# The folded rope weights of a decoder layer: block-structured 128x128 matmuls against four 64x64 tiles of the TensorE array

## The reference, cut to what matters

```python
q_hk = (hidden_q @ Wq.T).reshape(B, S, H=16, K=128)
q_big = einsum('bshk,hkq->bshq', q_hk, w_kc_q)            # 192 wide for each head
q_big = q_big * cos_q + rotate_half(q_big) * sin_q        # rotate_half: [-x[96:], x[:96]]
kv_r = kv_c * cos_k + rotate_half(kv_c) * sin_k           # 64 wide
q_r = einsum('bshq,hqr->bhsr', q_big, W_qr)               # 64 wide
k_r = einsum('bld,hdr->bhlr', kv_r, W_kr)
attn = softmax(einsum('bhsr,bhlr->bhsl', q_r, k_r))
ctx_c = einsum('bhsl,bld->bhsd', attn, kv_r)              # then w_kc_kv and Wo
```

## Time and profile before

| | us |
|---|---|
| median of 3 runs | 937.31 (935.73 to 937.69) |
| the profiled execution | 935.39 |
| its span, first to last instruction | 933.6 |

### The profile page before, as it was taken

How to read it: one execution, slowest core, us unless ns; L and a number is a source line. 1 busy time by engine, 2 the same in 40 slices (tenths; PEclk the granted TensorE clock), 3 DMA queues, 4 the chain that set the end, 5 groups by cost and what they waited for, 6 DMA issues and landing times.

```text
span 933.6 us, 12240 instructions
## 1 busy us (share of the span) xinstructions
PE 879.8 (94%) x4304; PEld 680.2 (73%) x4304; DVE 672.5 (72%) x1422; ACT 279.8 (30%) x498; POOL 170.7 (18%) x134
## 2 busy tenths in 40 slices
PE   5999999998999999999988899999999999999994
PEld 4966677764786657866655778888888888888873
DVE  3576886898868897778968786656666666666557
ACT  4421143110432103311145432323232323233232
POOL 4025600345003451024612200000000000000021
PEclk9999999999999999999999999999999999999997
DMA  9310000000000100000040014010212011000001
GB/s 296 129 35 0 1 2 1 31 16 16 0 0 0 45 14 1 1 1 24 3 144 35 23 20 153 24 73 1 78 42 54 19 58 55 18 10 1 1 23 68
DMA packets 16611, 35.35 MB, mean 38 GB/s; under 512 B 5681, under 2 KB 6577, under 8 KB 16177
## 3 DMA queue, kind: packets, MB, share of 16 engines
q1 hardware_dynamic: 16560, 34.72, 10.9%
HBM read 30.07 MB, written 2.36 MB: 35 GB/s over the span
## 4 chain that ended last, share of the span: by engine, by line
PE 42%; DVE 6%; issue 2%; ACT 0%; POOL 0%; ACTq 0%; DVEq 0%
PE ps L240 13%; PE ps L242 13%; PE ps L241 13%; DVE small L252 1%; PE ps L1465 1%; DVE fst L465 1%; PE ps L1456 1%; DVE hc L503 0%; DVE x2T_all L489 0%; DVE small L258 0%; PE ps L1431 0%; DVE su L497 0%; DVE fsm L256 0%; DVE small L1079 0%; PE ps L1441 0%
## 5 line engine op out<-in xcount | busy, mean ns | idle before, releaser
L497 DVE TENSOR_TENSOR su<-sg,ps 128x512 f32<-128x512 f32 x96 | 66.0, 687 | 132.9 <-PE ps L242 131.7
L1024 DVE TENSOR_TENSOR prod<-ps,ropeq 128x512 f32<-128x512 f32 (+1 forms) x224 | 142.5, 683 | 14.1 <-PE ps L242 12.3
L732 POOL TENSOR_TENSOR roped<-prod 128x512 f32<-128x512 f32 x96 | 121.8, 1283 | 164.0 <-DVE prod L1024 163.6
L240 PE MATMUL ps<-y_hi,f_hi 128*128 128x512 f32 x384 | 150.1, 391 | 0.0
L242 PE MATMUL ps<-y_hi,f_lo 128*128 128x512 f32 x384 | 149.5, 389 | 0.0
L241 PE MATMUL ps<-y_lo,f_hi 128*128 128x512 f32 x384 | 149.4, 389 | 0.0
L367 ACT ACTIVATE sg<-ps 128x512 f32<-128x512 f32 x96 | 57.4, 598 | 262.7 <-PE ps L242 262.7
L1392 PE MATMUL ps<-roped,m_w 128*128 128x512 f32 x192 | 91.9, 604 | 9.7 <-POOL roped L732 7.0
L240 PE MATMUL ps<-xT_hi,a_hi 128*128 128x512 f32 x192 | 84.5, 440 | 2.8 <-DVE xT_lo L949 2.8
L242 PEld LDWEIGHTS ps<-y_hi,f_lo 128*128 128x128 f32 x384 | 72.1, 188 | 15.1
L241 PEld LDWEIGHTS ps<-y_lo,f_hi 128*128 128x128 f32 x384 | 72.1, 188 | 14.9
(11 more groups left out here) (157 smaller groups left out, 1399.2 us busy)
## 6 DMA issues: line engine op xcount, KB each, us to landing
cb<-routing SPq DMA_DIRECT2D x32, 256.0 KB
f_raw<-in_L_ffn_gate_up_proj SPq DMA_DIRECT2D x8, 768.0 KB, 5.2
f_raw<-in_L_ffn_down_proj SPq DMA_DIRECT2D x8, 384.0 KB, 6.0
xb<-in_x SPq DMA_DIRECT2D x4, 512.0 KB, 3.8
lq<-in_L_xattn_Wq SPq DMA_DIRECT2D x1, 2048.0 KB, 13.2
x2T_all<-in_L_xattn_Wo SPq DMA_DIRECT2D x1, 2048.0 KB, 12.2
x2T_all<-x2T SPq DMA_DIRECT2D x4, 512.0 KB, 3.4
out<-res SPq DMA_DIRECT2D x4, 512.0 KB, 2.6
```

The source lines that it names most:

```text
L240: pe.matmul(dst, l_hi, r_hi, start=first, stop=False, skip_group_check=check)
L497: dve.tensor_tensor(su[:, k % 2], sg[:, k % 2], bank(2 * (k % 2) + 1), ALU.mult).then_inc(s_su, 1)
L732: pool.tensor_tensor(roped[:, p % 2, k], prod[:, 2 * k], prod[:, 2 * k + 1], ALU.add)\
L1024: return dve.tensor_tensor(t64(prod[o, dst, :]), t64(ps[r, src, :]), ropeq[r, table, :].unsqueeze(1).broadcast_to((r.stop - r.start, SEQS, ...
```

## The change

The rows of q_big are put in another order, so that k = 0 holds [0:64] of both heads, k = 1 [96:160] of both, and k = 2 the remaining [64:96, 160:192] of both, head h always in partitions 64h to 64h+63. For k = 2 the rotation of the halves is moved into the weights: m has a fourth piece, k = 3, with the rows of k = 2 in swapped order, and the two products of k = 2 go straight into `roped[:, p % 2, 2]` and `roped[:, p % 2, 3]`, without a GpSimd add. LQ(p) becomes 16 matmuls of 64x64 weights and 256 columns, on four tiles of the array (row half = head h, column half = h xor token half); its result lies in banks 6 and 7 (2 and 7 for p = 7), a half each, and is copied by four ACTIVATEs of 64x256. So all LQs share their banks. `fold_m` makes the same tiles directly, and `fold_a` has two matmuls for three. The logits and transposes of the block before, `shift_logits`, exp and `route` move by a place to later pairs and other banks.

```diff
-    m_w = sb(att, "m_w", [P, PAIRS, 3 * P])
+    m_w = sb(att, "m_w", [P, PAIRS, 4 * DC])
...
+    m_bank = lambda g, h: 4 + (g + h) % 2
+    q_bank = lambda p, h: (6 if p < PAIRS - 1 else 2, 7)[h]
...
-        sp.wait_ge(s_zero, 1)
-        for dst, src in (
...
-        ):
-            sp.dma_start(dst, src).then_inc(s_raw2, 16)
+        sp.dma_start(x2f[:, 0:2048], a["L0_xattn_W_qr"]).then_inc(s_raw2, 16)
+        sp.dma_start(x2f[:, 2048:2560], a["L0_xattn_W_kr"]).then_inc(s_raw2, 16)
...
-        sp.wait_ge(s_mps, PAIRS)
+        sp.wait_ge(s_mps, PAIRS // 2)
...
-        pool.memset(x2f, 0.0).then_inc(s_zero, 1)
...
-                for k in range(3):
+                for k in range(2):
                     pool.wait_ge(s_rp, 24 * b + 3 * p + k + 1)
...
-            for p in range(PAIRS):
-                act.wait_ge(s_mps, p + 1)
-                act.activation(m_w[:, p, :], ps[:, 4 + p % 2, 0:384], ACT.Copy).then_inc(s_m, 1)
+            for g in range(PAIRS // 2):
+                act.wait_ge(s_mps, g + 1)
+                for h in range(2):
+                    act.activation(m_w[64 * h:64 * h + 64, 2 * g:2 * g + 2, :],
+                                   ps[64 * h:64 * h + 64, m_bank(g, h), :].rearrange("p (r n) -> p r n", r=2),
+                                   ACT.Copy).then_inc(s_m, 1)
...
-                act.activation(lq[:, p], bank(6 + p % 2), ACT.Copy).then_inc(s_lq, 1)
+                for h in range(2):
+                    for th in range(2):
+                        r = 64 * (h ^ th)
+                        ins = act.activation(lq[64 * h:64 * h + 64, p, 256 * th:256 * th + 256],
+                                             ps[r:r + 64, q_bank(p, h), 0:256], ACT.Copy)
+                ins.then_inc(s_lq, 1)
                 if later and p == 0:
-                    x2T_out(b - 1, 3, 7)
+                    x2T_out(b - 1, 3, 2)
                     act.activation(x1[:], xn[:], ACT.Copy).then_inc(s_x1c, 1)
+                if later and p == 2:
                     act.wait_ge(s_lsub, b)
                     act.activation(rt[:, 1], rt[:, 0], ACT.Exp).then_inc(s_lexp, 1)
...
                     else:
+                        if p >= 2:
+                            dve.wait_ge(s_qr, 8 * b + p - 1)
                         dve.wait_ge(s_q, 24 * b + 3 * p + 3)
-                        times(4, f + 2, 4)
-                        times(5, f + 2, 5, slice(64, 128), slice(0, 64))
-                        times(5, f + 2, 5, slice(0, 64), slice(64, 128)).then_inc(s_rp, 1)
+                        times(roped[:, p % 2, 2], f + 2, 4)
+                        times(roped[:, p % 2, 3], f + 2, 5).then_inc(s_rp, 1)
...
-                if later and p == 1:
+                if later and p == 2:
                     shift_logits(b - 1, LOGITS)
-                if later and 2 <= p < 5:
-                    route(b - 1, 2 * p - 4)
-                    route(b - 1, 2 * p - 3)
+                if later and 3 <= p < 6:
+                    route(b - 1, 2 * p - 6)
+                    route(b - 1, 2 * p - 5)
...
         def fold_m():
-            pe.wait_ge(s_raw2, 8 * 16)
...
+            pe.wait_ge(s_raw2, 2 * 16)
+            for g in range(PAIRS // 2):
+                if g >= 2:
+                    pe.wait_ge(s_m, 2 * g - 2)
+                for p in (2 * g, 2 * g + 1):
+                    for k in range(4):
+                        for h in range(2):
+                            r = slice(64 * h, 64 * h + 64)
+                            o = (p % 2 * 4 + k) * DC
+                            mm = pe.matmul(ps[r, m_bank(g, h), o:o + DC], l_qr[r, p, k, :], r_kr[r, p, :],
+                                           start=True, stop=True)
...
             def latent_q(p):
                 if p == 0:
                     pe.wait_ge(s_bdT, 2 * b + 2)
-                if p == 0 and later:
-                    pe.wait_ge(s_x2T, 4 * b - 1)
-                if p == 1 and later:
-                    pe.wait_ge(s_lsub, b)
-                if p >= 2:
-                    pe.wait_ge(s_lq, 8 * b + p - 1)
-                for k in range(3):
-                    pe.wait_ge(s_rope, 24 * b + 3 * p + k + 1)
-                    mm = pe.matmul(bank(6 + p % 2), m_w[:, p, k * P:(k + 1) * P], roped[:, p % 2, k, :],
-                                   start=k == 0, stop=k == 2)
+                if p >= 1:
+                    pe.wait_ge(s_lq, 8 * b + p)
+                for k in range(4):
+                    if k < 2:
+                        pe.wait_ge(s_rope, 16 * b + 2 * p + k + 1)
+                    elif k == 2:
+                        pe.wait_ge(s_rp, 24 * b + 3 * p + 3)
+                    if k < 3:
+                        pe.nop(nofuse=True)
+                    for h in range(2):
+                        for th in range(2):
+                            i = slice(64 * h, 64 * h + 64)
+                            r = 64 * (h ^ th)
+                            mm = pe.matmul(ps[r:r + 64, q_bank(p, h), 0:256], m_w[i, p, k * DC:(k + 1) * DC],
+                                           roped[i, p % 2, k, 256 * th:256 * th + 256], start=k == 0, stop=k == 3)
                 mm.then_inc(s_qr, 1)
...
                 if later and p == 1:
-                    turn_x2(b - 1, 2, 6)
+                    turn_x2(b - 1, 2, 5)
...
+                if later and p == 2:
+                    turn_x2(b - 1, 3, 2)
+                if later and p == 3:
+                    logits(b - 1, LOGITS)
                 for k in range(3):
+                    if later and k == 2 and p in (1, 2):
+                        pe.wait_ge(s_x2T, 4 * b - 2 + p)
+                    if later and k == 2 and p == 3:
+                        pe.wait_ge(s_lsub, b)
...
-                if later and p == 2:
-                    logits(b - 1, LOGITS)
                 if p >= 1:
                     latent_q(p - 1)
-                if later and p == 1:
-                    turn_x2(b - 1, 3, 7)
```

76 lines of the change are left out of this document (32 added, 44 removed).

## The result

The changed kernel takes 914.87 us (median of 4 runs, 913.87 to 917.99) against 937.0 for the kernel before on the same chip. The ratio is 0.9767, 95% interval 0.9749 to 0.9784. On a second chip it took 914.63 against 937.75, ratio 0.9761 (0.9746 to 0.9775). The profiled execution took 914.6 us with a span of 912.6, 21.0 less than before.

A forecast was written before the change was run, and what follows sets the result against it. TensorE was taken to bound block 0 and part of block 3, VectorE's chain blocks 1 and 2. Terms -3.0 - 7.2 - 3.8 - 0.4 = -14.4 on 935.4 gave 921.0, with the median 1.9 higher 923 us; range 916 to 932.

The forecast's parts named there:

- LQ as four tiles: LQ in `pairs`: four records per 0.216 us slot, LQ from 2.57 to 2.07 us with mode changes, pair 6.68 to 6.18.
- The rival that row halves take turns: LQ on TensorE: 3.8 us instead of 2.57, TensorE bounds all stages, +32 us, 969 us; chance 0.12.
- strict program order: Skill's rule that matmuls start and end in order, making LQ 3.46 us; the prediction rejected it, citing `fold_u`.
- The products: VectorE in `pairs`: six products of 128 partitions take 3.65 us, 0.85 less per pair, bounds 0.65 to 0.90.
- The logits' later place: Blocks 1 and 2: logits ahead of A(3) and later small steps make VectorE idle 5.7 us instead of 2.55.
- `fold_a`: Weight folding: 0.65 us instead of 0.77 for each of 16 steps, -1.9 us.
- Block 3: Its `pairs`, bound by TensorE in part: A(7) 4.4 us earlier, copy 0.6 more, -3.8 us.
- Following the four lists in order ... and the durations above: Blocks 1 and 2, stepped through engine by engine: VectorE ends 3.5 us earlier, each stage -3.6, together -7.2.
- at the rate of L1431, 0.055 each: `fold_m`: 128 records take 7.0 us, 7.3 with the mode change, against 5.80 before: +1.5; the other end -2.0.
- copy 1.2 + 0.1: End of block 0: four ACTIVATEs copy LQ, 0.6 us more than one copy (bounds 0.5 and 0.95); block -3.0.
- That the issue of records bounds: Rival on TensorE: 0.055 us per record is the issue's rate, LQ costs 0.26 more, 929 us; chance 0.11.
- The clock at the stages' ends: Rival: TensorE's longer waits at pairs 6 and 7 of blocks 1 and 2 drop its clock, +5, 928 us; chance 0.06.

The follow-up runs named there:

- the load put back: Changed kernel plus, in each pair, one unread 128x512 GpSimd add behind the second one: 921.1 us, ratio to before 0.9824.
- product in halves: Changed kernel with each pair's last product as two VectorE operations on 64 partitions instead of one on 128: 920.24 us, ratio 0.9842.
- head by head: Changed kernel with LQ's sixteen matmuls ordered head, part, token half, all waits ahead of them: 946.22 us, ratio to before 1.0123.
- the one that folds half by half: Changed kernel with the folding's 64 matmuls ordered as eight records of one row half, then eight of the other: 916.71 us, ratio 0.9782.

## Why the prediction was wrong

**Right, in mechanism and size.** LQ as four tiles: 0.216 us for a slot of four records, 0.34 for the change of mode, a pair of 6.24. The rival that row halves take turns was wrong, and so was strict program order; a tile's two records follow each other in the program, and yet four records start within 0.02 us in the first slot, which I read as one for each tile. The products: 48 for a block of 0.68 us, 0.6 apart, 0.88 less for each pair (0.85 predicted). The logits' later place: VectorE idles 5.9 us in block 1 between its first product and its last (5.7 predicted, 2.55 before), in the brackets of these four rows of its timeline:

```profile
179.97 2.48 DVE L1028 TENSOR_TENSOR prod<-ps,ropeq 128x512 f32<-128x512 f32 x4 [0.66 <-PE ps L245]
185.11 0.29 DVE L1110 TENSOR_REDUCE rs<-ps 128x4 f32<-128x128 f32 x1 [1.47 <-PE ps L1348]
187.96 2.48 DVE L1028 TENSOR_TENSOR prod<-ps,ropeq 128x512 f32<-128x512 f32 x4 [2.23 <-PE ps L245]
193.16 0.29 DVE L1110 TENSOR_REDUCE rs<-rt 128x4 f32<-128x128 f32 x1 [1.52 <-ACT rt L835]
```

Also right: `fold_a`: -1.9, as predicted. Block 3, -3.74 against -3.8, is near in part by luck: its term for the copy was 0.4 short as in block 0 below, made up by the 0.2 that came from LQ(6) to the end of LQ(7), where the sum had nothing, and by some 0.1 ahead of it.

**The step that failed most: "Following the four lists in order ... and the durations above".** It took VectorE's small steps at the durations that they had before, while the same paragraph took away GpSimd's add of k = 2. The prediction has that add only as something that "leaves the end of the stage". It didn't ask which VectorE operation ran beside it. 3.4 us for each of blocks 1 and 2 were waits for it: in the kernel before without the add VectorE's steps lose 3.5, in the changed kernel with a like load they get 2.3 back and VectorE ends 2.1 later, and the same load on ScalarE lengthens none of them. Products -7.0, small steps -3.4, idle +3.3 make VectorE's end 7.0 earlier instead of 3.5. The tail, from there to `scores(0)`, grew by 0.6 where I had -0.1. The sum is -6.4 instead of -3.6, twice. (The 8 x 0.83 = 6.6 of the products should by the prediction's own 0.85 have been 6.8; they gave 7.0.) The folding's 2.5 more and block 0's 1.1 less make up the rest of the miss.

On this the Trainium skill, SBUF — State Buffer, Who interferes with whom, says that VectorE and GpSimd share a pair of ports that one of them holds for its whole instruction while the other waits, and that it is wanted by a VectorE instruction with two inputs in SBUF, against a GpSimd instruction that reads SBUF, and by copies and tensor_scalars in a two-port mode. The traces agree: the operations that wait are ones with two inputs in SBUF and tensor_scalars on four columns, and they end 0.02 to 0.15 us behind GpSimd's, while the products, with one input in PSUM, keep 0.68 us beside the adds. No trace shows in which mode a tensor_scalar ran. ScalarE's extra copies left the durations as they were, as the same section has it.

**`fold_m` "at the rate of L1431, 0.055 each", the upper end.** The term was mis-sized, 7.3 us against 4.8. Two records of 64 columns share a slot of about 0.058, 0.03 for each. I took the upper end because no row showed a faster rate, though the rate of L1431 came from records twice as wide. Half of it, the other end of my own bounds, was 3.8: the result lies at 4.8 because of two stops for the copies of `m_w`, 0.6 and 0.3, which I had counted as hidden.

**Block 0, "copy 1.2 + 0.1".** Three terms, 0.3 to 0.4 each. A(7) ended 2.7 earlier, not 3.0, since a pair became 0.45 shorter and not 0.50. From LQ(6) to the end of LQ(7) 0.2 came instead of 0.55: LQ(7) waits 1.76 us behind LQ(6), for its copy, where I had 1.6 with emptying. And the four copies come 0.39 apart, not 0.27, and take 1.55 us, 0.95 more than the one (the bounds, 0.5 and 0.95, held it; the sum had 0.6). The tail behind LQ(7) went from 1.3 to 2.2 us. Sharing the copy gave back 0.5 to 1.1 for each block.

**The rivals.** That the issue of records bounds: not at 0.055, since `fold_m` goes at 0.03. The clock at the stages' ends: in the changed kernel the granted clock is 1.00 in blocks 1 and 2, with waits of 0.26 and 0.57 us at LQ(6). But the mechanism is real and near: with a wait of 2.18 (the load put back) or 1.82 (product in halves) there it fell, for 1.3 us. The range: its lower end, 916, was the sum less a few us for the folding. It held nothing for a gain that I hadn't thought of, and the misses that counted, blocks 1 and 2 and the folding, were on that side.

What stays open: how far ahead TensorE looks for a record that can start (six records on, as in the changed kernel's LQ, is near enough; sixteen on, head by head, mostly isn't), why the clock's first rise comes when it does, and why it falls behind a wait of 0.79 us in one kernel and not behind the same wait in another.

## What to carry to other kernels

Before an operation on GpSimd is removed or moved, look in the trace at what VectorE does in the same microseconds: a small operation many times its usual length that ends with GpSimd's is part of the price of the GpSimd one. Then take these waits out of the durations before adding up. Read the granted clock of every stage that two profiles are compared by: three of the differences above would be put down to the wrong cause without it. With tiles of the array, put the matmuls of different row and column halves next to each other in the program, part by part, not head by head. And once the engine that sets the pace is relieved, sum the next one too: here VectorE gave 2.4 us and TensorE let 1.2 through.

## What the runs showed of the hardware

- Four 64x64 tiles of float32 matmuls run together at 0.216 us for four records of 256 columns, each tile's two records one behind the other (the trace doesn't name the tile; that is how the starts, four within 0.02 us, read); in another order of the same matmuls only two (1.96 against 2.87 us for an LQ).
- Beside a GpSimd add of 1.27 us, VectorE's operations with two inputs in SBUF and its tensor_scalars on four columns take up to 1.29 us instead of 0.15 to 0.26; products with an input in PSUM (0.68) and reductions (0.28) keep their time.
- VectorE needs 2.2 us from its last operation ahead of a loop's way back to its first behind it (0.56 for the same pair of operations with the way back ahead of both). This is free where the engine idles, and was 1.5 us where it didn't.
- TensorE's granted clock fell to 0.50 in LQ(6) of blocks 1 and 2 where TensorE had waited 1.8 to 2.2 us ahead of it, but not in every such block (product in halves: block 2 alone), and at LQ(1) of one kernel behind 0.79. The same 24 records then take 2.84 us instead of 1.53.
- TensorE's first matmuls, of 512 columns, start 0.43 us apart and last 0.63, later 0.23 and 0.39, the two levels of 1.2 and 2.4 GHz. The profile's rows give a granted clock of 1.00 for this stretch all the same, since the record of the granted clock begins with the rise: at 15.0 us in the kernel before, at 15.1 and 17.7 in the two executions of the changed one, at 18.2 at the latest, always with the same idle 1.5 us ahead of it. In the executions with a rise at 16.7 or later the clock also falls to 0.50 once between 54 and 62 us, behind a wait of 1.6; in those with a rise at 15.8 or earlier it doesn't. This moves the start by 1.3 us and block 0 by 0.6. The changed kernel:

```profile
14.69 0.57 PE L243 MATMUL ps<-xT_hi,w_hi 128*128 128x512 f32 x1
15.10 0.40 PE L244 MATMUL ps<-xT_lo,w_hi 128*128 128x512 f32 x1
```

and the one that folds half by half:

```profile
16.82 0.63 PE L245 MATMUL ps<-xT_hi,w_lo 128*128 128x512 f32 x1
```
